# A six-column coefficient table, spare products at the stage borders, and 23 units in the first MLP of a vision tower

## The reference

```python
h = tokens(x)                                     # 196 patches of 768 numbers @ W, class token, positions
h = h + attn0(layernorm(h))                       # 64 queries, 133 keys, one head; proj_w, proj_b
h = h + ffn0(layernorm(h))                        # gelu MLP 192 -> 768 -> 192, weights times coefficients
h = h + attn1(layernorm(h))                       # 12 heads of 64, over the 197 tokens of an image
h = h + ffn1(layernorm(h))                        # gelu MLP with quantised weights and activations
```

```python
for i, e in enumerate([96, 144, 192]):
    m_in = (d_idx < e)
    for j, r in enumerate([2, 3, 4]):
        a = alpha_e[i] * alpha_r[j]
        m_out = (h_idx < r * e)
        C0 += a * m_out[:, None] * m_in[None, :]   # 768 x 192
        c0b += a * m_out;  C1 += a * m_in[:, None] * m_out[None, :];  c1b += a * m_in
W0 = w_fc * C0;  b0 = b_fc * c0b;  W1 = w_proj * C1;  b1 = b_proj * c1b
```

## Time and profile before

| what | us |
|---|---|
| median of 3 runs (2645.07 to 2645.44) | 2645.27 |
| the profiled execution's own time | 2642.03 |
| its span in the profile | 2640.2 |
| embed_attend, 0 to 397.6: PE busy, DVE busy | 325.33, 271.95 |
| mlp_0, 397.6 to 802.5: PE busy, DVE busy | 380.58, 326.08 |
| attention_1, 802.5 to 2403.6: PE busy, DVE busy | 1576.89, 1392.52 |
| mlp_1, 2403.6 to 2640.2: PE busy, DVE busy, ACT busy | 176.06, 207.85, 213.78 |

### The profile page before, as it was taken

The page is one execution under the profiler, slowest core; times in us unless marked ns, Lnnn a source line. Parts: engine busy times, 40 slices in busy tenths (PEclk is TensorE's granted clock), DMA queues, the critical chain, the costliest instruction groups (busy, mean ns, idle before and its releaser), DMA issues. The chain is left out here.

```text
span 2640.2 us, 83428 instructions
## 1 busy us (share of the span) xinstructions
PE 2458.9 (93%) x27552; PEld 2112.2 (80%) x27552; DVE 2198.4 (83%) x5761; ACT 2094.3 (79%) x6199; POOL 1084.7 (41%) x1501
## 2 busy tenths in 40 slices
PE   5889977999997999999999999999999999996876
PEld 4778865877885888888888888888888888885665
DVE  6776768988776888888888888888888888887997
ACT  3677766777765888888888888888888888887998
POOL 5777732333331343443443333333334434341333
PEclk9999978999998999999999999999999999999999
DMA  5334400010002333333333333333333333330111
GB/s 172 110 104 117 119 19 25 0 40 5 0 0 56 81 73 69 83 69 69 83 69 72 80 71 73 76 76 73 71 80 71 69 83 69 69 83 10 45 43 51
DMA packets 181839, 173.22 MB, mean 66 GB/s; under 512 B 19206, under 2 KB 180432, under 8 KB 181520
## 3 DMA queue, kind: packets, MB, share of 16 engines
q1 hardware_dynamic: 181776, 172.44, 27.6%
HBM read 46.49 MB, written 9.68 MB: 21 GB/s over the span
## 5 line engine op out<-in xcount | busy, mean ns | idle before, releaser
L1349 POOL TENSOR_TENSOR b_pr<-b_pr,b_rinv 128x394 f32<-128x394 f32 (+1 forms) x768 | 625.0, 840 | 990.5 <-DVE b_rinv L1307 990.5
L1244 ACT ACTIVATE b_pr<-b_banks,b_nmx 128x197 f32<-128x197 f32 (+1 forms) x1536 | 626.8, 423 | 37.2 <-DVE b_nmx L1301 28.9
L1301 DVE TENSOR_REDUCE b_nmx<-b_banks 128x2 f32<-128x394 f32 (+1 forms) x768 | 395.7, 557 | 64.1 <-PE b_banks L1170 60.3
L1154 PE MATMUL b_banks<-b_xt,wqkv 128*128 128x197 f16 x3840 | 384.8, 250 | 4.8 <-DVE b_xt L1272 2.2
L1154 PEld LDWEIGHTS b_banks<-b_xt,wqkv 128*128 128x128 f16 x3840 | 318.4, 98 | 36.3 <-issue 18.9
L1180 PE MATMUL b_bank_t<-ident,b_pr 128*128 128x128 f32 (+3 forms) x3072 | 333.3, 250 | 5.4 <-DVE b_pt L1272 4.6
L1170 PE MATMUL b_banks<-b_kst,b_qst 128*128 128x197 f16 (+1 forms) x3072 | 326.5, 248 | 3.3 <-DMA b_kst<-b_qk 1.8
L1244 ACT ACTIVATION_READ_ACCUMULATOR b_pr<-b_banks,b_nmx 128x1 f32 (+1 forms) x1536 | 312.4, 203 | 0.0
L1180 PEld LDWEIGHTS b_bank_t<-ident,b_pr 128*128 128x128 f32 (+3 forms) x3072 | 287.0, 141 | 25.1 <-issue 10.8
L1170 PEld LDWEIGHTS b_banks<-b_kst,b_qst 128*128 128x128 f16 (+1 forms) x3072 | 264.8, 105 | 22.8 <-issue 11.0
L442 PE MATMUL tokens<-tok_w,parts 128*128 128x192 f16 (+1 forms) x2304 | 212.5, 254 | 57.2 <-POOL parts L314 57.2
(11 more groups left out here) (235 smaller groups left out, 4843.7 us busy)
## 6 DMA issues: line engine op xcount, KB each, us to landing
b_qst<-b_qk SPq DMA_DIRECT2D x512, 147.8 KB, 2.6
b_kst<-b_qk SPq DMA_DIRECT2D x512, 73.9 KB, 2.3
patches<-in_x SPq DMA_DIRECT2D x64, 588.0 KB, 4.3
out<-z_res SPq DMA_DIRECT2D x32, 192.0 KB
...
```

Source lines behind the costliest of these rows:

```text
L1154: last = t.matmul(out[:, g * SEQ:(g + 1) * SEQ], w[:, (2 * n + g) * P:(2 * n + g + 1) * P], x, start=(j == 0), stop=(j == 4))
L1244: last = nc.scalar.activation(pr[n % 3][0:ROWS[c], c, e, :], banks[0:ROWS[c], c, e * SEQ:(e + 1) * SEQ], ACT.Exp, bias=nmx[n % 2][0:ROWS[c ...
L1301: v.reduce_max(nmx[n % 2][0:ROWS[c], c, :], banks[0:ROWS[c], c, 0:2 * SEQ].rearrange("p (e t) -> p e t", e=2), AX.X, negate=True).then_inc ...
L1349: last = nc.gpsimd.tensor_tensor(p, p, inv, ALU.mult)
```

## The change

Three things are changed.

**1. The coefficients of the first MLP.** The 768-column rows `g` and `coef` become rows of six columns, one for each stretch between two edges. One unit, `coefficients`, makes them in 18 instructions of 1 to 6 columns. The multiplication by them moves to the places where the weights are rounded: ACT's `high_fc(k)` copies six pieces of a row with the piece's coefficient as its scale (in rounds 3 and 4; one copy of both rows in round 7 before), DVE's `low_fc(k)` multiplies and subtracts six pieces. `mask_fc` is gone. All units hang behind a1, rounds 1 to 9 (before: rounds 1 to 11, and 2 to 4 behind a0 too).

**2. Spare products.** `keep_working` puts products on TensorE whose results nothing reads, 313 in all: 76 between the last steps of embed_attend and 22 at its end; 50 before mlp_0's first T, 10 and 14 before its first two U, 13 at its end; 36, 7 and 8 before attention_1's first x, q and s, 23 in its last image and 9 at its end; 42 before mlp_1's first turn_x and 3 before its first up. They have 384 columns in embed_attend and 394 elsewhere.

**3. Units of mlp_0.** Sixteen units become 23, in rounds 1 to 18, 22 to 25 and 28 (before 1 to 11, 14 to 17, 19). `split_bias` becomes `divide_bias`, `split_bias`, `pick_bias` in rounds 16 to 18. ACT's `scale_keys` is split in two (rounds 21, 22), its `high_qkv` go to rounds 23 to 26 of its own count (a step u works two pairs ahead), `high_wo` to 28; DVE's `low_qkv` to 22 to 25 and `low_wo` to 28. With units that late, no round of this stage is left to loop on DVE and ACT; they are written out.

```diff
+def keep_working(t, n, bank, w, x):
+    for _ in range(n):
+        t.matmul(bank, w, x, start=True, stop=True)
...
-    h, RAW_FROM, RAW_SIZE = S["h"], 14, 50 * 2 * D
+    h, RAW_FROM, RAW_SIZE = S["h"], 50, 13 * 2 * D
...
-        g = raw(P, 3, HID)
-        coef = raw(P, 2, HID)
+        EDGES = sorted({r * e for r in RATIO_CHOICES for e in EMBED_CHOICES})
+        SPANS = [slice(lo, hi) for lo, hi in zip([0] + EDGES, EDGES)]
+        part = raw(P, 3, len(EDGES))
+        coef = raw(P, 2, len(EDGES))
...
-                def high_fc():
-                    act.wait_ge(masked, 1)
-                    copy(S["fc"][:, 0], r_fc[:]).then_inc(weights_hi, 1)
+                def high_fc(k):
+                    def make():
+                        act.wait_ge(masked, 1)
+                        for n, span in enumerate(SPANS):
+                            last = nc.scalar.activation(S["fc"][:, 0, k, span], r_fc[:, k, span], ACT.Copy, scale=coef[:, k, n:n + 1])
+                        last.then_inc(weights_hi, 1)
...
-                rounds(act, ACT_ORDER, count, job, {"h1": {7: high_fc, 9: high_fp}}, first=2)
+                rounds(act, ACT_ORDER, count, job, {"h1": {3: high_fc(0), 4: high_fc(1), 6: high_fp}}, first=2)
...
+                last_steps = {("t", 4): 12, ("s", 3): 14, ("t", 3): 10, ("s", 2): 5, ("t", 2): 10, ("s", 1): 5, ("t", 1): 10, ("j", 1): 10}
...
+                    if isinstance(p, int) and (kind, count - p) in last_steps:
+                        pe.wait_ge(taken[0], count)
+                        work(last_steps[kind, count - p])
...
                 rounds(pe, PE_ORDER, count, job, first=2)
+                work(22)
...
-                def coefficient(i):
-                        for j, r in enumerate(RATIO_CHOICES):
-                            then(v.tensor_scalar(g[:, i, 0:r * e], g[:, i, 0:r * e], alpha[:, 3 + j:4 + j], None, ALU.add))
-                        then(v.tensor_scalar(g[:, i, :], g[:, i, :], alpha[:, i:i + 1], None, ALU.mult))
+                def coefficients():
+                    for j, r in enumerate(RATIO_CHOICES):
+                        for i, e in enumerate(EMBED_CHOICES):
+                            to = slice(0, EDGES.index(r * e) + 1)
+                            last = v.tensor_scalar(part[:, i, to], part[:, i, to], alpha[:, 3 + j:4 + j], None, ALU.add)
+                        then(last)
...
-                        then(v.tensor_tensor(S["fc"][:, 1, k], r_fc[:, k], S["fc"][:, 0, k], ALU.subtract))
+                        for n, span in enumerate(SPANS):
+                            last = v.scalar_tensor_tensor(out=S["fc"][:, 1, k, span], in0=r_fc[:, k, span], scalar=coef[:, k, n:n + 1],
+                                                          in1=S["fc"][:, 0, k, span], op0=ALU.mult, op1=ALU.subtract)
...
-                first_slot = {2: coefficient(1), 3: coefficient_sum(0), 4: hidden_columns}
-                second_slot = {1: coefficient(0), 2: coefficient(2), 3: coefficient_sum(1), 4: mask_fc, 5: mask_fc_bias, 6: mask_fp, 7: mask_fp_bias,
-                               8: low_fc(0), 9: low_fc(1), 10: low_fp, 11: means}
+                units = {1: coefficients, 2: hidden_columns, 3: mask_fc_bias, 4: mask_fp, 5: mask_fp_bias, 6: low_fc(0), 7: low_fc(1),
+                         8: low_fp, 9: means}
...
-                units = {1: scales, 2: invert_rows(0), 3: invert_rows(1), 4: invert_rows(2), 5: invert_rows(3), 6: divide_first, 7: divide_second,
-                         8: quantise(0), 9: quantise(1), 10: sum_second, 11: split_bias, 19: low_wo}
-                units.update({14 + n: low_qkv(n) for n in range(4)})
+                units = {1: scales, 2: invert_scale, 3: invert_rows(0), 4: invert_rows(1), 5: invert_rows(2), 6: invert_rows(3), 7: divide_first(0),
+                         8: divide_first(1), 9: divide_second(0), 10: divide_second(1), 11: limit(0), 12: limit(1), 13: quantise(0), 14: quantise(1),
+                         15: sum_second, 16: divide_bias, 17: split_bias, 18: pick_bias, 28: low_wo}
+                units.update({22 + n: low_qkv(n) for n in range(4)})
...
-                rounds(act, ACT_ORDER, count, job, {"u": {14: scale_keys, 20: high_wo, **{15 + n: high_qkv(n) for n in range(4)}}}, first=2)
+                rounds(act, ACT_ORDER, count, job, {"u": {21: scale_keys(0), 22: scale_keys(1), 28: high_wo, **{23 + n: high_qkv(n) for n in range(4)}}}, first=2)
...
+                        if not later(p):
+                            work(50, 0)
...
+                        if isinstance(p, int) and p < 2:
+                            if p:
+                                pe.wait_ge(gelu_made, HC * p - 3)
+                            work((10, 14)[p], 2 * p)
...
+                work(13, 0)
...
+                first_steps = {("x", 0): 36, ("q", 0): 7, ("s", 0): 8}
+                last_steps = {("t", 3): 8, ("t", 4): 6, ("t", 5): 3, ("w", 0): 6}
...
                 run(pe, PE_ORDER, step)
+                work(9, bank_t[:, 0])
...
+                    if isinstance(u, int) and u + b == 0:
+                        work(42)
...
+                    if isinstance(u, int) and u + b == 0:
+                        work(3)
```

93 lines of the change are left out of this document (57 added, 36 removed).

## The result

The changed kernel takes 2628.43 us in the median (2627.77 to 2630.38, 4 runs), the kernel before 2645.36 beside it (2645.07 to 2648.43): a ratio of 0.9935, 95% interval 0.9922 to 0.9948, or 16.9 us less (13.8 to 20.6). The forecast was 2627, in a range of 2617 to 2637.

What follows compares the result with a forecast made beforehand. Bounds: TensorE, nearly always busy in the long middle stages, elsewhere losing time to waits behind DVE units and half clock around idle gaps. Savings 5.3 + 5.9 + 4.2 + 2.6 + 0.4 = 18.4 off 2645.27 gave 2627 us, range 2617 to 2637.

Steps and rivals of the forecast that it cites:

- Coefficients, 5.3 forecast: Early embed_attend: fewer long DVE units, moved earlier, cut token-step delays by 6.3, less 1.0 for ACT; range 0 to 9.
- 18 x 0.20 = 3.6 us: Early embed_attend, DVE: the new coefficients unit's 18 short instructions take 0.20 us each, so it saves next to nothing.
- signs of being wrong: Whole change: wrong if the tail's clock falls, POOL's statistics wait stays at 15 us, or all mlp_0's D steps widen.
- The 1.0 taken off for ACT's pieces: Early embed_attend: ACT's twelve small pieces instead of one copy cost 1.0 us, bounded by 0 and 5.
- The first border, 5.9 forecast: Embed_attend's tail and mlp_0's start: full clock saves 5.2 - 2.1 + 0.7 + 2.1 = 5.9 us; range 2 to 8.
- mlp_0, 4.2 forecast: mlp_0: splitting `split_bias` over three rounds saves 2.9 of interval and 1.3 of D step, 4.2 us; range 3 to 8.
- The second border, 2.6 forecast: Border at 802.5 us: full clock saves 0.6 on x, about 1.5 on q, rest earlier DMA; range 0 to 4.
- The third border, 0.4 forecast: Border at 2403.6 us: spare products fit in idle time, ScalarE bounds the rest; 0.4 us saved, range -1 to +1.
- Spare products at half clock: Rival, all borders: spare products run at half clock and hold the work up, 2681 us; 4%.
- Borders that give nothing: Rival, stage borders: clock holds but the cross-engine chain refills the gaps; only coefficients and units count, 9 us, 2636; 12%.
- ACT instead of DVE: Rival, early embed_attend: ACT bounds it, its twelve pieces eat the 6.3 us; 2636, or 2641 if the border fails; 11%.
- The case "more": More than forecast: the four waits behind `low_qkv` go too, or the first interval becomes quiet; 2619 us, 15%.

Runs made afterwards that it cites:

- coef_only: Kernel before with only the six-column coefficients, ACT's pieces and the new unit places in embed_attend; 2644.81 us against 2647.47, ratio 0.999.
- even_rounds: Changed kernel with embed_attend's nine units in rounds 2, 4, ... 18 and ACT's copies in rounds 5, 7 and 11; 2625.47 us, ratio 0.9921 to before.
- after_again: The changed kernel itself, unaltered, measured and profiled once more in another group; 2629.74 us against 2647.76 for the kernel before, ratio 0.993.
- units_only: Kernel before with the 23 units of mlp_0 alone; 2639.46 us against 2647.47, ratio 0.9976.
- cold_fills: Changed kernel without the 76 and 22 spare products of embed_attend's tail; 2631.32 us against 2642.90 for the kernel before, ratio 0.9953.
- end_8: Changed kernel with 8 instead of 22 spare products behind embed_attend's last projection; 2625.33 us, ratio 0.9914 to before.
- fills_only: Kernel before with all 313 spare products and nothing else; 2634.84 us against 2647.47, ratio 0.9952.
- first_border: Kernel before with only the spare products from embed_attend's tail to mlp_0's first U's (76, 22, 50, 10, 14); 2634.38 us against 2642.90, ratio 0.997.
- low_qkv_late: Changed kernel with DVE's `low_qkv` one round later, in rounds 23 to 26; 2622.80 us against 2642.90 for the kernel before, ratio 0.9927.

## Why the prediction was right

The sum was 18.4 us; the segments give 3.1 + 5.9 + 4.9 + 1.9 - 0.2 = 15.6, and the timing 16.9. What makes up the other 1.3 isn't shown. The first border and mlp_0 came out by the steps that the forecast named; the early part came out smaller and not by its sum. Point by point:

- **Coefficients, 5.3 forecast, 3.1 measured,** and 2.7 by coef_only's timing, whose interval ends at 4.8. That DVE's long units in rounds 2 and 3 were the worst is borne out: their interval is 1.4 us too long instead of 6.3, POOL's wait behind them fell from 5.92 to 1.51. The sum built on it is not. The term "18 x 0.20 = 3.6 us" was too small: the unit took 4.6, so the wait ahead of step 5 grew by 1.5, which the forecast had at nothing, and step 5 comes 0.9 us later on the mean (40.7 against 39.8). That is taken off the 4.0 us gained from step 5 to 45. The six pieces of `low_fc` were left out of the sum too (an estimate of 2 us stood beside it): the two units took 4.9 us instead of 2.2, and the interval in which they stand lost 4.2 us instead of 2.3. That the losses add up to 11.6 against 11.8 is the luck of one profiled execution; the mean over the eight kernels with the table is 13.1, a gain of 4.0 where 6.3 was said. One of the forecast's own signs of being wrong came up: POOL's waits for the statistics stayed near 15 us (14.4), and even_rounds, which brought them to 5.6, took the same 134.0 us from step 5 to 29. So the whole of the early part doesn't hang on that wait. The 1.0 taken off for ACT's pieces was never measured by itself: POOL's waits for ACT's `parts`, from 20 to 180 us, went from 21.0 to 23.2, and no run leaves ACT's pieces out.
- **The price of an idle time.** The forecast read from the earlier trace rows that the clock falls behind 2.29 us of idle time and not behind 1.81. The later traces don't keep to it: in after_again the step at 63.03 takes 3.14 us behind 2.44, in units_only the one at 95.38 takes 4.80 behind 1.66, and in attention_1 half clock followed 1.76 us in some traces and not in others.
- **The first border, 5.9 forecast, 5.9 measured.** The full-clock rebuilding of the tail was a little high (5.2, measured 4.4), the price of the 22 products too (2.1, measured 1.7), T to D right (2.8 and 2.7). The 50 fitted, with 0.41 us to spare. cold_fills bears out the tail's term, end_8 that of the 22.
- **mlp_0, 4.2 forecast, 4.9 measured.** The long interval behind `split_bias` is gone as said. In the two profiled executions the gain is 5.5: the forecast's 4.2, 0.8 behind `low_wo` and 0.5 in small pieces, which the sum left out. The 1.3 of a D step at half clock was not there in every execution: of the four kernels with the old units, fills_only and first_border have none. The four waits of `low_qkv` stayed, as said, and low_qkv_late shows that they were worth 4.3, about what the range's upper end gave them.
- **The second border, 2.6 forecast, 1.9 measured.** x to s gave 1.7 in the two profiled executions, of which the products account for 0.6 and an earlier DMA for the rest. What was missing in the step is that the clock can still fall 30 us later.
- **The third border, 0.4 forecast, -0.2 measured,** within its range. "ScalarE is the bound behind it" held for turn_x and up, and the forecast didn't see that the clock then falls in the first down steps.
- **The rivals.** Spare products at half clock: cold_fills shows that they bring the clock back. Borders that give nothing: first_border excludes it. ACT instead of DVE: that the early part gains nothing is out by the segments of eight kernels against four, how much ACT's pieces take off it is untested. The case "more" would have needed the edit of low_qkv_late.
- **The sign and the range** stood on five parts worked out one by one. Three came out small (2.2, 0.7 and 0.6 us), one large (0.7) and one as said; that the time came out within 1.4 us of the forecast owes something to the 1.3 us that the segments don't hold.
